# A graph layer with attention and experts on one core: the order behind the adjacency products rewritten, router logits in a bank of their own, the bias adds moved, batches of four throughout

## What is computed

```python
xn = layernorm(x)
# graph branch: e = exp(w - max), attention = e / (row_sum[src] + 1e-6)
out0 = segment_sum(att * M[dst], src); out1 = segment_sum(att * M[src], dst)   # M = xn @ Wm + bm
h = relu(layernorm(concat(out0, out1) @ W1 + b1) * gamma + beta)
gnn = where(row_sum > 0, relu(h @ W2 + b2), 0)
# mixing branch: q, k = softmax per head, v; linear attention; out @ Wp.T + bp
x = x + gnn + mix(xn)
# experts: route = argmax(softmax(layernorm(x) @ Ws + bs)) over 8 experts
x = x + prob_max * expert[route](layernorm(x))          # gelu(x @ w1 + b1) @ w2 + b2
```

## Time and profile before

| | |
|---|---|
| median of 3 runs | 546.54 us (544.47 to 549.55) |
| the profiled execution | 546.23 us, span 544.4 us, mean clock 0.95 |
| chain that ended last, by engine | POOL 30%, PE 27%, DVE 23%, issue 10% |
| PE busy | 476.6 us (88%) |
| DVE busy | 412.8 us (76%) |
| ACT busy | 249.4 us (46%) |
| POOL busy | 198.1 us (36%), 118 scatters, 17 gathers, 17 output writes |

### The profile page before, as it was taken

The page is one execution under the profiler, slowest core; times in us unless marked ns, Lnnn a source line. Parts: engine busy times, 40 slices in busy tenths (PEclk is TensorE's granted clock), DMA queues, the critical chain, the costliest instruction groups (busy, mean ns, idle before and its releaser), DMA issues.

```text
span 544.4 us, 8877 instructions
## 1 busy us (share of the span) xinstructions
PE 476.6 (88%) x2825; PEld 376.1 (69%) x2825; DVE 412.8 (76%) x792; ACT 249.4 (46%) x666; POOL 198.1 (36%) x157
## 2 busy tenths in 40 slices
PE   4289999999979999889999999799977886799992
PEld 1167878888857879676666666699855565588881
DVE  6969999999969878989999998332254758355552
ACT  0485586655751100016666666542242255456550
POOL 0078878788877778600000000000000003545422
PEclk9799999999999999999999999899998666899998
DMA  7960000000000000040000000000004951423310
GB/s 193 316 222 3 2 2 3 2 3 3 1 1 3 3 1 3 3 172 1 2 1 2 2 1 2 1 0 1 1 0 183 420 204 25 133 91 102 97 63 15
DMA packets 15776, 31.08 MB, mean 57 GB/s; under 512 B 7686, under 2 KB 8317, under 8 KB 14709
## 3 DMA queue, kind: packets, MB, share of 16 engines
q1 hardware_dynamic: 9237, 23.21, 12.5%
q0 software_dynamic: 6496, 7.31, 7.0%
HBM read 24.90 MB, written 7.38 MB: 59 GB/s over the span
## 4 chain that ended last, share of the span: by engine, by line
POOL 30%; PE 27%; DVE 23%; issue 10%; DMA 4%; ACT 3%; SPq 1%; DVEq 0%; POOLq 0%; ACTq 0%
POOL slots L448 29%; DVE s_hot L1184 8%; PE banks L818 6%; DVE d_hot L1177 5%; PE banks L526 4%; PE banks L703 4%; DVE s_one L1173 3%; PE banks L720 3%; DMA rec<-in_x 3%; PE banks L696 2%; PE banks L761 2%; PE banks L683 2%; PE banks L809 1%; DVE rec L1190 1%; PE banks L745 1%
## 5 line engine op out<-in xcount | busy, mean ns | idle before, releaser
L448 POOL DMA_INDIRECT slots<-record,row_i x118 | 160.5, 1360 | 69.0 <-issue 41.8
L459 POOL DMA_INDIRECT rec<-x_rows,get_i x17 | 20.3, 1196 | 231.8 <-DVE get_i L1335 226.9
L683 PE MATMUL banks<-d_hot,s_hot 128*128 128x251 bf16 x648 | 92.0, 276 | 5.6 <-DVE s_hot L1184 5.6
L1502 ACT ACTIVATE adj<-banks x108 | 63.7, 589 | 42.6 <-PE banks L683 42.5
L683 PEld LDWEIGHTS banks<-d_hot,s_hot 128*128 128x128 bf16 x648 | 54.4, 98 | 14.9 <-issue 6.5
L526 PE MATMUL banks<-w_hi,xT_hi 128*125 128x512 f32 (+1 forms) x160 | 59.5, 372 | 0.8 <-DVE bia L1023 0.4
L526 PE MATMUL banks<-w_hi,xT_lo 128*125 128x512 f32 (+1 forms) x160 | 58.5, 366 | 0.0
L526 PE MATMUL banks<-w_lo,xT_hi 128*125 128x512 f32 (+1 forms) x160 | 58.5, 366 | 0.0
L1184 DVE TENSOR_TENSOR s_hot<-s_one,parts 128x1024 bf16<-128x1024 bf16 (+2 forms) x87 | 51.3, 639 | 0.0
L1447 ACT ACTIVATE q_sb<-q_sb,hmax 125x64 f32<-125x64 f32 x80 | 26.7, 335 | 39.7 <-DVE hmax L1042 39.7
L526 PEld LDWEIGHTS banks<-w_hi,xT_hi 128*125 128x125 f32 x160 | 29.7, 185 | 7.1 <-issue 1.6
(11 more groups left out here) (289 smaller groups left out, 1029.5 us busy)
## 6 DMA issues: line engine op xcount, KB each, us to landing
w_raw<-in_w2f SPq DMA_DIRECT2D x4, 1024.0 KB, 8.6
w_raw<-in_wqkv SPq DMA_DIRECT2D x3, 1024.0 KB, 18.7
rec<-in_x SPq DMA_DIRECT2D x2, 1120.0 KB
x_rows<-rec SPq DMA_DIRECT2D x10, 224.0 KB
w1a<-in_w1f SPq DMA_DIRECT2D x1, 2048.0 KB, 8.7
w1b<-in_w1f SPq DMA_DIRECT2D x1, 2048.0 KB, 15.8
b_sb<-in_b2f SPq DMA_DIRECT2D x1, 2048.0 KB, 21.0
slots<-record,row_i POOLq DMA_INDIRECT x118, 2.6
```

The lines of the kernel that those rows point to most:

```text
L448: pool.indirect_dma_start(slots, bass.IndirectOffsetOnAxis(ap=row_i[:, c:c + 1], axis=0), record[:, c, :], None).then_inc(slot_st, 16)
L459: pool.indirect_dma_start(rec_c[:, c % RING, :], None, x1_rows, bass.IndirectOffsetOnAxis(ap=get_i[:, c:c + 1], axis=0)).then_inc(ld_rec[c ...
L683: mm = pe.matmul(flat_banks[:, bass.ds(at_in, AW)], s_hot[:, n % DB, i, q, :, j], d_hot[:, n % DB, q, :, j], start=False, stop=(i == WT - ...
L1502: act.activation(adj[:, bass.ds(w, BW2)], flat_banks[0:TP, bass.ds(out_at, BW2)], ACT.Copy).then_inc(win_ok, 1)
```

## The change

- `PCOLS` is 50 instead of 52: 25 sorting steps instead of 26, 120 scatters instead of 118. `RUN_UP` (run-up products ahead of the chunks) is 18 instead of 16.
- `BATCHES` are 26 of four pairs and two of two, where they were 1, 1, 2 and 26 of four. PE waits for batch n alone, where it waited for three (`LEAD`) before the first pair.
- The ten bias adds leave the batch loop and stand in the loop over tiles beside the inward products.
- `rinv_ok` is given by the reciprocal itself, ahead of `valid`.
- The exponents of the edge weights are ACT's first instruction.
- The tail of PE and ACT is written in another order; the logits lie in bank 6, and `route` no longer waits for `hidT_ok`. For tiles 4 to 7 (`DA`, `DZ`) ACT subtracts the mean (`x2_centre`, `x2_act`) instead of DVE, which writes the negated mean.

```diff
-PCOLS = 52
+PCOLS = 50
-PB, DB, LEAD = 4, 4, 3
+PB, DB = 4, 4
-RUN_UP = 16
+RUN_UP = 18
+DA, DZ = 4, 8
-BATCHES = [(0, 1), (1, 2), (2, 4)] + [(i, min(i + PB, PAIRS)) for i in range(4, PAIRS, PB)]
+BATCHES = [(i, i + PB) for i in range(0, PAIRS - PB, PB)] + [(PAIRS - PB, PAIRS - 2), (PAIRS - 2, PAIRS)]
...
-                    pe.wait_ge(batch_ok, max(n + 1, LEAD))
+                    pe.wait_ge(batch_ok, n + 1)
...
             def x2_turn(t):
-                pe.wait_ge(x2_ok, t + 1)
+                if DA <= t < DZ:
+                    pe.wait_ge(x2_act, t - DA + 1)
+                else:
+                    pe.wait_ge(x2_ok, t + 1 if t < DA else t + 1 - (DZ - DA))
...
             def route(t):
                 pe.wait_ge(x2T_ok, t + 1)
-                pe.wait_ge(hidT_ok, min(t // 2 + 3, NW))
                 for k in range(KD):
-                    mm = pe.matmul(bank[1][0:TP, 256 + t * E:256 + (t + 1) * E], x2T[:, t % 2, k, :], ws[:, k, :],
+                    mm = pe.matmul(bank[6][0:TP, t * E:(t + 1) * E], x2T[:, t % 2, k, :], ws[:, k, :],
...
-            for w in range(NW + 3):
...
+            for w in range(NW):
+                outward(w, 0)
+                if w >= 1:
                     hid_turn(w - 1)
+                if w == NW - 1:
+                    both(x2_turn, 0)
+                outward(w, 1)
+                if w >= 2:
+                    both(hid_out, w - 2)
+                if w >= 1:
                     hid_back(w - 1)
+            hid_turn(NW - 1)
+            both(route, 0)
+            both(x2_turn, 1)
+            both(hid_out, NW - 2)
+            hid_back(NW - 1)
+            both(route, 1)
+            both(x2_turn, 2)
+            both(hid_out, NW - 1)
+            both(route, 2)
+            both(x2_turn, 3)
+            both(route, 3)
+            both(x2_turn, 4)
+            both(route, 4)
...
-                if n >= 7 and n % 2 == 1 and (n - 7) // 2 < NT:
-                    t = (n - 7) // 2
-                    dve.wait_ge(mix_ok, t + 1)
-                    dve.tensor_tensor(rec[:, t, :], rec[:, t, :], bias("p"), ALU.add).then_inc(bp_ok, 1)
...
+            own_step(dve.tensor_scalar(rse[:, :], rs[:, :], 1e-6, None, ALU.add))
+            dve.reciprocal(rinv[:, :], rse[:, :]).then_inc(rinv_ok, 1)
             dve.tensor_scalar(valid[:, :], rs[:, :], 0.0, None, ALU.is_gt)
...
                     if n % 2 == 1:
                         turn_copy(n)
+                dve.tensor_tensor(rec[:, t, :], rec[:, t, :], bias("p"), ALU.add).then_inc(bp_ok, 1)
...
+                if DA <= t < DZ:
+                    own_step(dve.bn_aggr(mv[:, t, :], stat[:, t, :]))
+                    dve.tensor_scalar(nmr[:, t:t + 1], mv[:, t, 0:1], -1.0, None, ALU.mult).then_inc(var2_ok, 1)
+                    return
...
+            act.wait_ge(ld_w, 32)
+            act.wait_ge(top_sb, 1)
+            act.activation(record[:, :, 1], wraw[:, :], ACT.Exp, bias=top[:, 3:4]).then_inc(w_exp, 1)
             act.wait_ge(ld_x[1], 32)
...
+            def x2_centre(t):
+                act.wait_ge(var2_ok, t + 1)
+                act.wait_ge(x2T_ps, t - 1)
+                act.activation(xn[:, t % 2, :], rec[:, t, :], ACT.Identity, bias=nmr[:, t:t + 1]).then_inc(x2_act, 1)
```

More of the change, by code:

```diff
@@ L767, in _, with both @@
             pe.wait_ge(turn_v, 15)
-            for w in range(NW + 3):
-                if w < NW:
-                    outward(w, 0)
-                if 1 <= w < NW + 1:
-                    hid_turn(w - 1)
[L773 to L778, removed]
-                    hid_back(w - 1)
[L780 to L784, removed]
+            def both(step, w):
+                step(2 * w)
+                step(2 * w + 1)
+            for w in range(NW):
+                outward(w, 0)
+                if w >= 1:
+                    hid_turn(w - 1)
+                if w == NW - 1:
[4 more added lines that the diff above has]
+                if w >= 1:
+                    hid_back(w - 1)
+            hid_turn(NW - 1)
[11 more added lines that the diff above has]
+            both(route, 4)
             pe.wait_ge(oh_ok, 1)
@@ L1186, in _ @@
                 last.then_inc(batch_ok, 1)
[L1187 to L1190 removed]
             dve.wait_ge(win_ok, PAIRS)
             own_step(dve.tensor_reduce(rs[:, :], adjw[:, :, :, WIN], X, ALU.add))
+            own_step(dve.tensor_scalar(rse[:, :], rs[:, :], 1e-6, None, ALU.add))
+            dve.reciprocal(rinv[:, :], rse[:, :]).then_inc(rinv_ok, 1)
             dve.tensor_scalar(valid[:, :], rs[:, :], 0.0, None, ALU.is_gt)
[L1196 to L1198 removed]
+            dve.wait_ge(rinv_ok, 1)
             def turn_copy(n):
@@ L1212, in _ @@
             scale_adj(1)
+            dve.wait_ge(mix_ok, NT)
+            dve.wait_ge(row_ok, 1)
             for t in range(NT):
@@ L1283, in _ @@
             dve.wait_ge(log_ps, NT)
-            own_step(dve.tensor_tensor(logit[:, :, :], bank[1][0:TP, 256:256 + NT * E].rearrange("p (t e) -> p t e", t=NT),
+            own_step(dve.tensor_tensor(logit[:, :, :], bank[6][0:TP, 0:NT * E].rearrange("p (t e) -> p t e", t=NT),
                                        over_e(rstd[:, :]), ALU.mult))
@@ L1392, in _ @@
             act.activation(mv[:, DT:NT, 1], x_sum[:, 2, :], ACT.Copy, scale=1.0 / D).then_inc(var_ok, 1)
-            act.wait_ge(ld_w, 32)
-            act.wait_ge(top_sb, 1)
-            act.activation(record[:, :, 1], wraw[:, :], ACT.Exp, bias=top[:, 3:4]).then_inc(w_exp, 1)
             def high_part(i):
@@ L1561, in _, with both @@
             act.wait_ge(ld_small, 16)
-            for w in range(1, NW + 3):
-                if w < NW + 1:
-                    hid_copy(w - 1)
-                    hid_std(w - 1)
-                    hid_relu(w - 1)
-                if 2 <= w < NW + 2:
-                    relu(2 * w - 4)
-                    relu(2 * w - 3)
-                if w >= 3:
-                    x2_copy(2 * w - 6)
-                    x2_copy(2 * w - 5)
+            def x2_centre(t):
+                act.wait_ge(var2_ok, t + 1)
+                act.wait_ge(x2T_ps, t - 1)
+                act.activation(xn[:, t % 2, :], rec[:, t, :], ACT.Identity, bias=nmr[:, t:t + 1]).then_inc(x2_act, 1)
+            def both(step, w):
+                step(2 * w)
+                step(2 * w + 1)
+            hid_copy(0)
+            for w in range(1, NW):
+                if w == NW - 1:
+                    both(x2_copy, 0)
+                hid_std(w - 1)
+                hid_copy(w)
+                if w == NW - 1:
+                    hid_relu(w - 1)
+                if w >= 2:
+                    both(relu, w - 2)
+                if w < NW - 1:
+                    hid_relu(w - 1)
+            both(x2_copy, 1)
+            hid_std(NW - 1)
+            x2_centre(4)
+            hid_relu(NW - 1)
+            x2_centre(5)
+            both(relu, NW - 2)
+            both(x2_copy, 2)
+            both(x2_centre, 3)
+            both(relu, NW - 1)
+            both(x2_copy, 3)
+            both(x2_copy, 4)
             act.wait_ge(var2_ok, NT)
```

7 lines of the change are left out of this document (2 added, 5 removed).

## The result

The changed kernel takes 521.76 us (median of four, 521.37 to 528.79) where the kernel before took 548.04 us beside it (544.47 to 549.65): a ratio of 0.9563, 95% interval 0.9481 to 0.9645, some 24 us. The ratio is worked out from the single executions, a fifth one of 524.38 us among them, and not from the two medians, which lie 26.3 us apart. The forecast was 525.1 in a range of 519.5 to 531.5. Run again with the experiments it took 524.55 (520.98 to 525.04), ratio 0.9550 (0.9499 to 0.9602). These eight executions have their median at 523.2. Four executions of this case were in a slower state and are left out of the ratios: 553.30 us of the kernel before, 678.79 of the one with 52 columns, and 547.98 of the batches alone and 554.40 of the exponents alone, which were the profiled ones, so that no step's time is read from those two profiles.

A forecast was written before the change was run, and what follows sets the result against it. No engine bounds the whole; stages do in series: scatters, DVE's batches, PE's waits in the tail. 6.5 us from scatters, batches and `rinv_ok` plus 14.9 from the tail make 21.4, giving 525.1 us, range 519.5 to 531.5.

The forecast's parts named there:

- Scatters and table: POOL's scatters: start 3.3 us earlier, two more cost 3.0; 0.4 us gained, bounds 3.0 later to 1.5 earlier.
- the second scatter's row: Scatter of 2.53 us instead of 1.19 beside a DVE subtraction; forecast to hit another scatter, not one more.
- Batches: DVE's one-hot batches feeding PE's pairs: 5.2 us of stalls given back, 0.8 us at the first pair.
- Bias adds: Ten adds, 6.0 us of DVE, hidden in its idle time beside the inward products; cost nothing, bound 0 to 6 us.
- Inward stage: First transposes to first outward product; forecast unchanged, still 36 us with ten adds in DVE's gaps.
- a sign of being wrong: Prediction wrong if the inward stage grows, or if PE's waits only move to other rows of the tail.
- The rival of a stall at every tile: Adds delay DVE's copies beside inward products, PE stalls, clock halves all stage: 32 us lost, 557 us; chance 0.03.
- The tail: First outward product to last logit: 68.0 us to 53.1 by PE's new order, 14.9 gained, bounds 10 to 17.9.
- The rival of the tile chain: Each tile's chain over DVE and ACT bounds the tail, half of 14.9 us lost: 532.5 us; chance 0.07.
- The separate bank: Logits' own bank removes route's wait for hidT_ok, never last before but last in the new order.
- Transfers: Expert weights' transfers, started by hid_ps, drain before the first gather with 5.7 us of cover left of 13.
- The rival of late transfers: Expert weights land after the gather needs them, cover short by as much as 4 us: 529 us; chance 0.04.

The follow-up runs named there:

- the one with 52 columns: Changed kernel with 52 columns sent as a list instead of 50, so 118 scatters and one sorting step more; 522.72 us, ratio 0.9526.
- the batches alone: Kernel before with only batches of four, PE waiting for one batch, and the bias adds moved beside the inward products; ratio 0.9877.
- the exponents alone: Kernel before with only the exponents first and 50 columns instead of 52; ratio 0.9988.
- The padded old order: Kernel before, old tail order, with 15 extra unused products inside PE's waits for the centred tile and x2_copy; 541.13 us, ratio 0.9861.

## Why the prediction came out right

**Scatters and table** (-0.4 in the sum; +0.5 and -2.2 measured). The start came as said, at 24.65 and 24.25 for 24.9, and the last issue at 229.82 and 227.20 for 228.6. The table's +0.5 lies inside my bounds and its -2.2 a little beyond the 1.5 that I allowed, and the arithmetic of 1.49 us a scatter does not carry to tenths: gaps of 2.3 us and more in POOL's issue (below) and scatters beside long DVE operations move the end by 2.6 us from one execution to the next. The run with 52 columns shows what the step lacked: I said that the sort and the longer run-up end ahead of the first batch. In the profile of 528.79 us they do, by 1.0 us; in the other the run-up ends last, and 1.2 us of the table's 2.2 are lost to it.
My reading of the second scatter's row held: it no longer meets the subtraction of 128x2048; the fourth does, at 29.29, and takes 3.17 us, and the one at 26.30, beside DVE's statistics, takes 1.20. It hits another one, not one more: ten scatters of over 2 us before, ten after. The Trainium skill (SBUF — State Buffer, the part on "DVE blocks DMA") states such a stall of descriptors written by GpSimd for DVE operations in a 2-port mode; here the operation beside the slow scatter is a subtraction of two arrays in SBUF, so the delay is measured and the reason that the page gives is not.

**Batches** (-5.2 and -0.8; measured -4.8 in both profiles, and -0.7 and +0.5, the latter where the run-up ended last). 107 pairs in 95.45 us are 0.892 each for my 0.888. The last -0.1, for `rinv_ok`, measured the same.

**Bias adds** (0; 0). The adds cost nothing where they are and 3.0 us where they were.

**Inward stage** (0; +1.1 and +1.0). I had named a growth of this stage as a sign of being wrong, and it grew, by the clock and not by the adds: the ten transposes took 2.43 us for 1.44 before, and DVE's copies and adds held nobody up. With the adds moved and full clock the stage is 32.16, 1.7 shorter than before. The rival of a stall at every tile needed a clock of 0.50 over the stage; it was 0.91. What decides whether the gap ahead of the transposes ends in half clock is open.

**The tail** (-14.9; -16.3). PE's waits are 2.7 us for my 4.4, and of half clock the last rows have about 3: 1.6 in the last router steps, 1.3 in the eight transposes ahead of them (2.32 for 1.05) and 0.3 in the step before; the estimate was 3. The padded old order supports a part of the term's reason. Summing the tail's rows over what they take at full clock, I estimate half clock at 10.7 us in the old tail, 6.0 in the padded one and 3.3 in the changed one: by that, filled waits give back 4.7 us and the new order 7.4, where I had reckoned with 12.4 - 3 = 9.4; the waits gave 7.2 for my 5.5, and 1.7 of the 16.3 are in neither. The padded tail has 4.2 us of wait left, about what I forecast for the new order, and still twice its half clock, so the waits alone do not explain it; what else does is open. "3 us" was a choice between two values, and that it came within a few tenths, and that the two parts were off in opposite directions, is luck. What the step got wrong is who sets the pace. I carried durations through three queues and found PE's order to be the bound, with waits on DVE and ACT at four places, of which three came (1.16, 0.49 and 1.05 us for 1.1, 0.7 and 1.3); in the trace DVE is the fuller engine from 404 to 423, and 1.4 us put on it move its last centred tile by 1.3. The rival of the tile chain was near to this but put the tail at 60 us; the amount of DVE's work bounds it at 52.
The separate bank was costed as taking away a wait that would come last in the new order. It would: by 1.26 us, at the first two pairs.

**Transfers** (0, with 5.7 us of cover; +0.4 and +0.7). They are issued 27.55 us into the tail where it was 34.82, the 7.2 us earlier that I forecast; 403.12 for my 400 comes from a tail that began 2.5 us later than forecast in this profile. The step that I left out is the store of the factors: I held the drained transfers against the gather alone, and the store, issued at 430.02 while they are under way, takes 6.69 us and lands 0.4 us behind the list of indices. The rival of late transfers had this mechanism, but its price was 0.4 to 0.7 us, not 4.

**What the sum left out.** Gather to end was 89.2 us in one profile and 86.4 in the other, against 87.0 before, and nothing in it was edited. Of the 4.2 us between the two spans, 2.8 are there, 2.7 at the table, less 1.2 between table and first pair. The eight executions lie 8 us apart, and the unedited stages make up a good part of that; no step of mine carried it, so that a forecast 3.3 and 0.6 us from the two medians is closer than its working warrants. Some of that is luck in the starting point too: I took 21.4 us from a median of 546.54, while the kernel before took 548.0 to 549.0 beside the changed one, and the gain by ratio is 24. Two slips in the working of the range did no harm: the best case's 8.1 should be 8.0 by my own terms, and the worst case of 533.4 that I worked out lies outside the 531.5 that I gave.

## What to carry over

Waits on an engine in order can cost TensorE's clock beside their own length (3.9 us of the old tail came back when they were only filled): read the granted clock of the stretch beside the waits, and count it as a term of its own. After a reordering that removes waits, look for the engine that has become full; here DVE did over 19 us, and the next gain there is to be sought in its work rather than in PE's order. Before a change of 1 us in a step is put down to an edit, look how far the same step varies in kernels that leave it alone. Where two paths end within a microsecond of each other, as the sort's run-up and the scatters' table do, shortening one of them is worth nothing measurable.

## What the hardware showed that I had not expected

POOL's queue of indirect scatters pauses before the 40th, the 79th and the 118th, whatever kernel: 2.40, 2.31 and 2.29 us in the kernel before (the last stands as issue time in the earlier trace rows), 3.53, 2.30 and 2.28 in the changed one (the first is 2.38 to 4.06 over all profiles), against 0.30 or 0.31 ahead of the others. With 118 scatters the third pause falls on the very last one. I took it for a single wait at the end. Why it comes every 39 scatters no run here shows.

Filling waits with work that nobody uses paid in one kernel and not in the other: 15 extra products made the old one 1.4% faster (0.7 to 2.1%), and 26 of them made the changed one neither faster nor slower.
